# A two-layer graph network on one core: 391 edge tiles in place of 392, and gathers spread differently among the scatters

## The chip, the cores and the metric

The kernel runs on one core of a Trainium2 chip. The metric is the device time of one execution in microseconds. The kernel before has a median of 2975.88 us over three runs (2974.57 to 2979.17).

## The reference

A graph with 100000 nodes of 64 features and 50000 edges, sorted by their target `dst`. Two layers, each with a residual and a layer norm:

```python
def _L0_gnn_ref(features, src, dst, edge_weight, W1, W2, b1, b2):
    messages = features[src] * edge_weight[:, None]
    aggregated = jax.ops.segment_sum(messages, dst, num_segments=N_NODES)
    act = lambda x: jax.nn.leaky_relu(x, negative_slope=LEAKY_ALPHA)
    out = act(features * aggregated @ W1 + b1) + act(aggregated @ W2 + b2)
    sq = jnp.sum(out * out, axis=1, keepdims=True)
    return out * jax.lax.rsqrt(jnp.maximum(sq, L2_EPS))

def _L1_gnn_ref(x, edges, edge_weights, ...):
    node_indices, neighbour_indices = (edges[0], edges[1])
    messages = _ffn(x[neighbour_indices], W1p, b1p, W2p, b2p) * edge_weights[:, None]
    agg = jax.ops.segment_sum(messages, node_indices, num_segments=num_nodes)
    out = _ffn(jnp.concatenate([x, agg], axis=1), W1u, b1u, W2u, b2u)
    sq = jnp.sum(out * out, axis=-1, keepdims=True)
    return out * jax.lax.rsqrt(jnp.maximum(sq, EPS_L2))

edge_index = jnp.stack([src, dst])
x = _layernorm(x + _L0_gnn_ref(x, src, dst, ...), axis=-1)
x = _layernorm(x + _L1_gnn_ref(x, edge_index, edge_weight, ...), axis=-1)
```

The first layer gathers by `src` and adds by `dst`; the second gathers by `dst` and adds by `src`.

## The kernel before

**Tiles and windows.** A tile is 128 edges, one a partition. Four tiles (WT) are a window. 50000 edges fill 390 tiles (EC) and 80 edges of one more, so 391 tiles hold edges; the kernel rounds up to 98 windows (NWIN), 392 tiles. Windows are counted from 0 to 97 here, tiles from 0 to 391. The padding edges of the last tile carry weight 0 and are scattered to rows outside the result. Node rows are worked in chunks of 1024 (CR), also 98 (NCH).

**Three stages**, each a block with a barrier at its end. `first_edges` makes the edge sums of the first layer. `second_edges` computes the first layer's node rows, 8 groups of a chunk and the 4 gathered tiles of a window together, and from the latter the messages and edge sums of the second layer. `last_rows` computes the second layer's node rows.

**First edge stage.** POOL sends one indirect DMA for each tile (`gather`, line 243), which fetches 128 rows of x into the big tile `xg`. DVE builds matrices `weigh` that join edges of a window with the same target (`equal_rows`, lines 368 and 374), PE applies them (`join`, line 300), ACT evicts the sums into a ring of three buffers `ms` (`take`, line 323), and POOL adds them to the table in HBM with one accumulating indirect DMA for each tile (`scatter`, line 256). Scatter k waits for take k and for the landing of scatter k-1 (all four DMAs); take k waits for the landing of scatter k-3. Before its loop, POOL sends EARLY = 112 gathers and waits until SP's DMAs have cleared the table (`zeroed3`). Then it runs through the windows: scatter k, and then the gathers from upto(k) to upto(k+1):

```python
def upto(k):
    return min(EARLY + (TILES - EARLY) * k // (NWIN - 4), TILES)
```

PE's join k waits for the gathers of its window, which are counted in pairs of windows after the first 28 (`arrival`).

**Second edge stage.** POOL sends the gathers of 8 windows (LEAD), then for each k scatter k (line 546) and the four gathers of window k+8 (line 532), as long as there are any. A gather fills a slot of the ring `box` (6 slots, SB), and the first of a window waits until the slot's former rows are added. The other engines work in rounds; in round t:

```python
for t in range(ROUNDS):
    of(t, 2, sum_outputs)
    ...
    of(t, 2, sum_centred)
    of(t, 0, multiply)
```

is DVE's list, where `of(t, lag, what)` does window t-lag. `multiply` (line 731) is the first step on a window: it waits for the window's gathers and for SP's load of the chunk. PE turns and multiplies it one round later, and the window's take (line 691) comes five rounds after. So take k and multiply k+4 are near each other in time, and take k needs multiply k+3. Here too take k waits for the landing of scatter k-3, and scatter k for take k and for the landing of scatter k-1.

Of the kernel before, what the change touches and what calls it, by code (L numbers as in the profile page):

```python
# [39 lines left out]
def gnn_kernel(nc, x, src, dst, edge_weight, w1a, w2a, b1a, b2a, w1p, b1p, w2p, b2p, w1u, b1u, w2u, b2u, out):  # L40
# [6 lines left out]
    assert EC < TILES  # L47
# [5 lines left out]
    EARLY = 28 * WT  # L53
# [29 lines left out]
    with ctx:  # L83
# [42 lines left out]
        def first_edges():  # L126
            c = ExitStack()
            with c:
# [30 lines left out]
                def arrival(k):  # L159

                    if k < COARSE:
                        return k // 4, 16 * WT * 4
                    pair = (k - COARSE) // 2
                    of = min(2, NWIN - COARSE - 2 * pair)
                    return COARSE // 4 + pair % RING, 16 * WT * (2 * (pair // RING) + of)
# [22 lines left out]
                with nc.Block(no_gpsimd_drain=True) as block:  # L188
# [52 lines left out]
                    def _(pool):  # L241
# [35 lines left out]
                        pool.wait_ge(scattered, 16 * TILES)  # L277
# [67 lines left out]
                    def _(dve):  # L345
# [96 lines left out]
        def second_edges():  # L442
            c = ExitStack()
            with c:
# [48 lines left out]
                with nc.Block(no_gpsimd_drain=True) as block:  # L493
# [31 lines left out]
                    def _(pool):  # L525
                        def gather(i, h):

                            if h == 0:
                                wait(pool, added, i - SB + 1)
                            for b in range(JOIN * h, JOIN * (h + 1)):  # L530
                                at = i * WT + b
                                pool.indirect_dma_start(out=box[i % SB][:, b, :, :].rearrange("p a f -> p (a f)"), out_offset=None,  # L532
                                                        in_=table_rows[:, :],
                                                        in_offset=bass.IndirectOffsetOnAxis(ap=node[1][:, at:at + 1], axis=0),
                                                        ).then_inc(gathered[i % SB], 16)

                        def scatter(k, h):
# [6 lines left out]
                            for b in range(JOIN * h, JOIN * (h + 1)):  # L544
                                at = k * WT + b
                                pool.indirect_dma_start(out=state[:, :], out_offset=bass.IndirectOffsetOnAxis(ap=sidx[1][:, at:at + 1], axis=0),  # L546
# [3 lines left out]
                        for i in range(LEAD):  # L550
                            for h in range(HALVES):
                                gather(i, h)
                        for k in range(NWIN):
                            for h in range(HALVES):
                                scatter(k, h)
                                if k + LEAD < NWIN:
                                    gather(k + LEAD, h)
                        for h in range(HALVES):
                            pool.wait_ge(scattered[h], 16 * JOIN * NWIN)
# [156 lines left out]
                    def _(dve):  # L716
# [326 lines left out]
```

## Time and profile before

| What | Value |
|---|---|
| Median of three runs | 2975.88 us |
| The profiled execution | 2982.28 us |
| its span in the profile | 2980.5 us |
| First edge stage | 0 to 1270 us |
| Second edge stage | 1273 to 2578 us |
| Last stage | 2580 to 2980 us |
| POOL, DVE, PE busy | 2361.0, 2211.5, 2150.9 us |

Times in the timeline are microseconds from the start of the span: the first number of a row is the start, the second the duration, and in brackets stands the idle time just before with what ended it. "issue" is a pause that nothing in the profile explains. POOL's duration of an indirect DMA is the making of its descriptors, not its landing; the landing shows in whoever waits for it. In the groups by line, a row gives busy time and mean nanoseconds of one, then the idle time before. In the windows, a row gives each engine's busy time and instructions in a stretch, the granted TensorE clock as a share of 2.4 GHz, and the DMA engines' share.

### The profile page before, as it was taken

The numbers are of one execution on the slowest core, as the hardware profiler recorded it, in microseconds if no ns is written. First come the engines' busy times: TensorE is split into PE (matmuls) and PEld (weight loads), VectorE is DVE, ScalarE is ACT, GpSimd is POOL, SyncE is SP. The second block draws the span as 40 slices with busy tenths as digits, with TensorE's granted clock in tenths as the row PEclk, the third lists the DMA queues.
The fourth block names the chain that finished last, engine by engine and source line by source line (L and its number), as shares of the span: only waits on it lengthen the run. The fifth ranks groups of instructions, "written<-read, shape, count | busy, mean of one in ns | idle before, by whom it ended". The sixth has DMA issues, their size and how long they took to land. (4 is left out here: it accounts for less than half of the span.)

```text
span 2980.5 us, 39234 instructions
## 1 busy us (share of the span) xinstructions
PE 2150.9 (72%) x11956; PEld 1675.4 (56%) x11956; DVE 2211.5 (74%) x5627; ACT 1070.7 (36%) x1964; POOL 2361.0 (79%) x1774
## 2 busy tenths in 40 slices
PE   4036555555555554269999999989999998599997
PEld 3035555555554544247777666666666666366664
DVE  5079888888888886457778777777777777188888
ACT  0000000000000000035555455545555554288887
POOL 7777888888888888758888888888888887488888
PEclk8555555555555555579999999999999999699998
DMA  9998888888888767467787777777777776356664
GB/s 228 206 204 187 180 173 177 175 183 177 176 180 170 158 141 151 83 175 179 186 187 184 169 166 176 180 176 159 178 178 169 170 175 123 79 196 207 206 209 156
DMA packets 1036087, 516.48 MB, mean 173 GB/s; under 512 B 540544, under 2 KB 998336, under 8 KB 1035880
## 3 DMA queue, kind: packets, MB, share of 16 engines
q1 hardware_dynamic: 764616, 372.57, 47.6%
q0 software_dynamic: 144256, 77.17, 19.2%
q10 hardware_dynamic: 127008, 64.23, 7.6%
q8 instruction: 99, 1.62, 0.2%
q14 instruction: 108, 0.88, 0.1%
HBM read 269.97 MB, written 243.84 MB: 172 GB/s over the span
## 5 line engine op out<-in xcount | busy, mean ns | idle before, releaser
L300 PE MATMUL sums<-xg,weigh 128*128 128x64 f32 x1960 | 437.7, 420 | 514.8 <-ACT ms L323 358.7
L546 POOL DMA_INDIRECT state<-ms,sidx x392 | 630.8, 1609 | 145.2 <-issue 116.9
L256 POOL DMA_INDIRECT table<-ms,sidx x392 | 622.2, 1587 | 142.2 <-issue 115.5
L300 PEld LDWEIGHTS sums<-xg,weigh 128*128 128x128 f32 x1960 | 423.2, 329 | 548.6 <-issue 471.5
L368 DVE TENSOR_SCALAR weigh<-rowp,key,ew 128x128 f32<-128x128 f32 (+3 forms) x784 | 423.9, 602 | 167.9 <-PE rowp L288 160.7
L532 POOL DMA_INDIRECT box<-table,node_dst x392 | 401.9, 1025 | 130.0 <-issue 107.6
L243 POOL DMA_INDIRECT xg<-in_x,node_src x392 | 382.8, 976 | 120.8 <-issue 104.9
L323 ACT ACTIVATE ms<-sums 128x256 f32<-128x256 f32 x98 | 37.6, 384 | 1144.4 <-DMA table<-ms,sidx 1076.1
L374 DVE SCALAR_TENSOR_TENSOR seen<-rowp,key,earlier 128x128 f32<-128x128 f32 (+3 forms) x784 | 383.1, 544 | 0.0
L579 PE MATMUL z_p<-turned_s,wz 128*128 128x512 f32 x588 | 331.7, 647 | 24.9 <-ACT turned_s L652 20.8
L589 PE MATMUL o_p<-cenz,leaky 128*128 128x65 f32 x2352 | 285.1, 278 | 27.6 <-DVE leaky L737 27.2
L589 PEld LDWEIGHTS o_p<-cenz,leaky 128*128 128x128 f32 x2352 | 272.9, 193 | 48.3 <-DVE leaky L737 48.2
L288 PE MATMUL rowp<-ident,key 128*128 128x128 f32 x784 | 186.4, 418 | 129.2 <-DVE seen L374 122.0
L625 PEld LDWEIGHTS ffo<-g,weigh_in 128*128 128x128 f32 x1960 | 238.3, 195 | 48.0 <-issue 47.3
L658 ACT ACTIVATE leaky<-z_p,bz 128x512 f32<-128x512 f32 x294 | 202.0, 687 | 129.6 <-PE z_p L579 119.3
L288 PEld LDWEIGHTS rowp<-ident,key 128*128 128x128 f32 x784 | 166.8, 241 | 129.9 <-DVE seen L374 122.8
L625 PE MATMUL ffo<-g,weigh_in 128*128 128x64 f32 x1960 | 234.4, 276 | 1.6 <-issue 1.6
L737 DVE SCALAR_TENSOR_TENSOR leaky<-z_p,bz,leaky 128x512 f32<-128x512 f32 x294 | 217.9, 741 | 21.6 <-ACT leaky L658 21.3
L570 PEld LDWEIGHTS turned_p<-ident,box 128*128 128x128 f32 x1176 | 154.6, 155 | 131.5 <-issue 80.3
L870 POOL TENSOR_TENSOR inv<-ssq,mhalf 128x8 f32<-128x8 f32 x98 | 161.0, 1642 | 74.4 <-DVE ssq L975 74.4
L570 PE MATMUL turned_p<-ident,box 128*128 128x128 f32 x1176 | 180.9, 296 | 48.0 <-DVE box L731 48.0
L742 DVE TENSOR_REDUCE v<-sq_y 128x12 f32<-128x768 f32 x98 | 93.4, 953 | 157.5 <-ACT sq_y L669 157.5
(94 smaller groups left out, 3549.6 us busy)
## 6 DMA issues: line engine op xcount, KB each, us to landing
box<-table SPq DMA_DIRECT2D x97, 768.0 KB, 5.3
joins<-weigh ACTq DMA_DIRECT2D x98, 640.0 KB, 3.8
weigh_in<-joins SPq DMA_DIRECT2D x98, 640.0 KB
table<-rows SPq DMA_DIRECT2D x97, 512.0 KB, 5.4
pair<-state SPq DMA_DIRECT2D x97, 512.0 KB, 3.8
xin<-in_x SPq DMA_DIRECT2D x97, 256.0 KB, 6.1
state<-y SPq DMA_DIRECT2D x97, 256.0 KB, 7.7
out<-y SPq DMA_DIRECT2D x97, 256.0 KB, 2.2
```

What stands on the lines that cost most here:

```text
L243: pool.indirect_dma_start(out=xg[:, i, :], out_offset=None, in_=x[:, :], in_offset=bass.IndirectOffsetOnAxis(ap=node[0][:, i:i + 1], axis= ...
L256: pool.indirect_dma_start(out=table[:, :], out_offset=bass.IndirectOffsetOnAxis(ap=sidx[0][:, i:i + 1], axis=0), in_=ms[k % MR][:, b, :], ...
L288: last = pe.transpose(rowp[n][k % 2][:, b * P:(b + 1) * P], key[n][:, i:i + 1].to_broadcast([P, P]), ident[:, :])
L300: last = pe.matmul(sums[k % 2][:, a * D:(a + 1) * D], block_of(0, k, b)[:, a * P:(a + 1) * P], xg[:, k * WT + b, :], start=b == a, stop=b ...
L368: last = dve.tensor_scalar(block_of(n, k, b), rowp[n][k % 2][:, (b + 1 - m) * P:(b + 1) * P], key[n][:, i:i + 1], ew[:, i:i + 1], ALU.is_e ...
L374: last = dve.scalar_tensor_tensor(out=seen[b][:, 0:m * P], in0=rowp[n][k % 2][:, (b + 1 - m) * P:(b + 1) * P], scalar=key[n][:, i:i + 1], ...
L532: pool.indirect_dma_start(out=box[i % SB][:, b, :, :].rearrange("p a f -> p (a f)"), out_offset=None, in_=table_rows[:, :], in_offset=bass ...
L546: pool.indirect_dma_start(out=state[:, :], out_offset=bass.IndirectOffsetOnAxis(ap=sidx[1][:, at:at + 1], axis=0), in_=ms[k % SM][:, b, :] ...
L570: last = pe.transpose(turned_p[n % 2][:, g * P:(g + 1) * P], box[i % SB][:, 4 * q + g, 0:2, :].rearrange("p a f -> p (a f)"), ident[:, :])
L579: pe.matmul(z_p[n % 2][:, :], wz[:, :], turned_s[q][:, :], start=True, stop=True).then_inc(z_up, 1)
L589: last = pe.matmul(o_p[:, b, g * M8:(g + 1) * M8], leaky[i % 2][r // 4][:, r % 4 * P:(r % 4 + 1) * P], cenz[:, :], start=True, stop=True)
L625: last = pe.matmul(ffo[:, (WT + a) * D:(WT + a + 1) * D], weigh[i % SW][:, at * P:(at + 1) * P], g2[i % 2][:, b * D:(b + 1) * D], start=b ...
```

## The change

The last tile, which holds no edges, is neither gathered nor scattered in either stage (`FILLED` = 391, `MISSING` = 1). The semaphore counts that wait for it are lowered. Its place in `xg` is set to zero by one DVE memset at the start of the kernel. EARLY goes from 112 to 120. In the first stage `upto` divides by NWIN - 3 in place of NWIN - 4, and in the second stage, which sent all four gathers of window k+8 after scatter k, a like `upto` spreads the remaining 359 gathers over 92 windows in place of 90.

```diff
+    FILLED = EC + (ER > 0)
+    MISSING = TILES - FILLED
...
-    EARLY = 28 * WT
+    EARLY = 30 * WT
...
-                            return min(EARLY + (TILES - EARLY) * k // (NWIN - 4), TILES)
+                            return min(EARLY + (TILES - EARLY) * k // (NWIN - 3), FILLED)
...
-                            for b in range(WT):
-                                i = k * WT + b
+                            for i in range(k * WT, min((k + 1) * WT, FILLED)):
+                                b = i % WT
...
+                        if MISSING:
+                            dve.memset(xg[:, FILLED:TILES, :], 0.0)
...
-                        def gather(i, h):
-
-                            if h == 0:
+                        def gather(at):
+
+                            i, b = divmod(at, WT)
+                            if b == 0:
                                 wait(pool, added, i - SB + 1)
...
+                        def upto(k):
+                            return min(LEAD * WT + (FILLED - LEAD * WT) * k // (NWIN - 6), FILLED)
...
                         for k in range(NWIN):
                             for h in range(HALVES):
                                 scatter(k, h)
-                                if k + LEAD < NWIN:
-                                    gather(k + LEAD, h)
+                            for at in range(upto(k), upto(k + 1)):
+                                gather(at)
...
-                            dve.wait_ge(gathered[s], 16 * WT * (i // SB + 1))
+                            dve.wait_ge(gathered[s], 16 * (WT * (i // SB + 1) - (MISSING if i == NWIN - 1 else 0)))
```

The end of POOL's list in the first stage, from scatter 93 on, before. A row is a run of equal instructions; xg is filled by gathers, table by scatters:

```order
199 L256 DMA table<-ms_0,sidx 300640x64 x4
200 L243 DMA xg<-in_x,node_src 128x64 x3
201 L256 DMA table<-ms_1,sidx 300640x64 x4
202 L256 DMA table<-ms_2,sidx 300640x64 x4
203 L256 DMA table<-ms_0,sidx 300640x64 x4
204 L256 DMA table<-ms_1,sidx 300640x64 x4
```

The same place now:

```order
199 L259 DMA table<-ms_0,sidx 300640x64 x4
200 L246 DMA xg<-in_x,node_src 128x64 x3
201 L259 DMA table<-ms_1,sidx 300640x64 x4
202 L246 DMA xg<-in_x,node_src 128x64 x2
203 L259 DMA table<-ms_2,sidx 300640x64 x4
204 L259 DMA table<-ms_0,sidx 300640x64 x4
205 L259 DMA table<-ms_1,sidx 300640x64 x3
```

Two gathers stand after scatter 94, where none stood; scatters 95, 96 and 97 end the list, and the last has three DMAs. In the loop 14 windows are followed by two gathers (0, 7, 14, 21, 29, 36, 43, 51, 58, 65, 73, 80, 87, 94), where two were (0 and 47); the others by three.

The end of POOL's list in the second stage, from scatter 88 on, before; box is filled by gathers, state by scatters:

```order
384 L546 DMA state<-ms_1,sidx 200640x64 x4
385 L532 DMA box<-table,node_dst 128x192 x4
386 L546 DMA state<-ms_2,sidx 200640x64 x4
387 L532 DMA box<-table,node_dst 128x192 x4
388 L546 DMA state<-ms_0,sidx 200640x64 x4
389 L546 DMA state<-ms_1,sidx 200640x64 x4
390 L546 DMA state<-ms_2,sidx 200640x64 x4
391 L546 DMA state<-ms_0,sidx 200640x64 x4
392 L546 DMA state<-ms_1,sidx 200640x64 x4
393 L546 DMA state<-ms_2,sidx 200640x64 x4
394 L546 DMA state<-ms_0,sidx 200640x64 x4
395 L546 DMA state<-ms_1,sidx 200640x64 x4
```

And now, from scatter 89 on:

```order
387 L555 DMA state<-ms_2,sidx 200640x64 x4
388 L536 DMA box<-table,node_dst 128x192 x4
389 L555 DMA state<-ms_0,sidx 200640x64 x4
390 L536 DMA box<-table,node_dst 128x192 x4
391 L555 DMA state<-ms_1,sidx 200640x64 x4
392 L536 DMA box<-table,node_dst 128x192 x4
393 L555 DMA state<-ms_2,sidx 200640x64 x4
394 L555 DMA state<-ms_0,sidx 200640x64 x4
395 L555 DMA state<-ms_1,sidx 200640x64 x4
396 L555 DMA state<-ms_2,sidx 200640x64 x4
397 L555 DMA state<-ms_0,sidx 200640x64 x4
398 L555 DMA state<-ms_1,sidx 200640x64 x3
```

The last gathers stand after scatter 91 in place of 89. To fill those two places, windows 0, 10, 20, 30, 40, 51, 61, 71 and 81 are followed by three gathers, so that each gather stands 1 (after window 0) to 9 tiles (after window 81) later in the list than before.

## Rows read from the trace of the kernel before

**Rows 1.** The page, busy time of each engine.

```profile
PE 2150.9 (72%) x11956; PEld 1675.4 (56%) x11956; DVE 2211.5 (74%) x5627; ACT 1070.7 (36%) x1964; POOL 2361.0 (79%) x1774
```

**Rows 2.** Windows: busy time in two stretches of the second edge stage.

```profile
1400.00:1600.00 200.00, 189.54 (x1209) 144.06 (x1209) 159.61 (x361) 109.53 (x200) 161.42 (x124) 1.00 0.79 183
...
2545.00:2555.00 10.00, 8.44 (x30) 6.27 (x29) 0.00 (x0) 1.63 (x4) 6.80 (x5) 0.50 0.28 16
```

**Rows 3.** Groups by line: POOL's gathers and scatters of both stages.

```profile
L546 POOL DMA_INDIRECT state<-ms,sidx x392 | 630.8, 1609 | 145.2 <-issue 116.9 <-DMA state<-ms,sidx 15.2 <-ACT ms L691 13.1
L256 POOL DMA_INDIRECT table<-ms,sidx x392 | 622.2, 1587 | 142.2 <-issue 115.5 <-DMA table<-ms,sidx 9.7 <-ACT ms L323 8.8
L532 POOL DMA_INDIRECT box<-table,node_dst x392 | 401.9, 1025 | 130.0 <-issue 107.6 <-DMA state<-ms,sidx 11.3 <-DVE y L780 8.5
L243 POOL DMA_INDIRECT xg<-in_x,node_src x392 | 382.8, 976 | 120.8 <-issue 104.9 <-DMA table<-ms,sidx 14.3 <-DMA node_src<-in_src 1.6
```

**Rows 4.** Timeline of POOL: the last early gather and the first scatter.

```profile
143.39 0.95 POOL L243 DMA_INDIRECT xg<-in_x,node_src  x1 [0.31 <-issue]
152.56 1.64 POOL L256 DMA_INDIRECT table<-ms,sidx  x1 [8.23 <-DMA table<-zeros]
```

**Rows 5.** Timeline of POOL around window 47, and ACT's take of window 50.

```profile
702.98 1.55 POOL L256 DMA_INDIRECT table<-ms,sidx  x1 [0.30 <-issue]
...
706.16 0.98 POOL L243 DMA_INDIRECT xg<-in_x,node_src  x1 [0.30 <-issue]
708.29 1.62 POOL L256 DMA_INDIRECT table<-ms,sidx  x1 [1.14 <-ACT ms L323]
...
707.57 0.38 ACT L323 ACTIVATE ms<-sums 128x256 f32<-128x256 f32 x1 [11.75 <-DMA table<-ms,sidx]
```

**Rows 6.** Timelines: last scatter of window 68, and ACT's take of window 71.

```profile
942.35 1.55 POOL L256 DMA_INDIRECT table<-ms,sidx  x1 [0.30 <-issue]
...
946.81 0.39 ACT L323 ACTIVATE ms<-sums 128x256 f32<-128x256 f32 x1 [11.63 <-DMA table<-ms,sidx]
```

**Rows 7.** Timelines: last gather, PE's join of window 96, first bare gap.

```profile
1233.45 0.95 POOL L243 DMA_INDIRECT xg<-in_x,node_src  x1 [0.30 <-issue]
...
1240.39 1.55 POOL L256 DMA_INDIRECT table<-ms,sidx  x1 [0.30 <-issue]
1244.26 1.55 POOL L256 DMA_INDIRECT table<-ms,sidx  x1 [2.32 <-DMA table<-ms,sidx]
...
1236.99 4.50 PE L300 MATMUL sums<-xg,weigh 128*128 128x64 f32 x20 [16.54 <-issue]
```

**Rows 8.** Timelines of POOL and DVE: a scatter and a multiply that meet.

```profile
1710.86 2.30 POOL L546 DMA_INDIRECT state<-ms,sidx  x1 [0.30 <-issue]
...
1710.71 0.95 DVE L731 TENSOR_TENSOR box<-box 128x768 f32<-128x768 f32 x1
```

**Rows 9.** Timeline of POOL: last gather of window 93, scatters 91, 92, 97 begin.

```profile
2449.75 1.32 POOL L532 DMA_INDIRECT box<-table,node_dst  x1 [0.30 <-issue]
...
2513.81 1.55 POOL L546 DMA_INDIRECT state<-ms,sidx  x1 [3.37 <-ACT ms L691]
...
2523.59 1.55 POOL L546 DMA_INDIRECT state<-ms,sidx  x1 [2.30 <-DMA state<-ms,sidx]
...
2571.15 1.55 POOL L546 DMA_INDIRECT state<-ms,sidx  x1 [2.40 <-DMA state<-ms,sidx]
```

**Rows 10.** Timelines: DVE's multiplies of windows 93 and 97, takes 90, 91, 97.

```profile
2465.72 0.95 DVE L731 TENSOR_TENSOR box<-box 128x768 f32<-128x768 f32 x1
...
2515.18 0.95 DVE L731 TENSOR_TENSOR box<-box 128x768 f32<-128x768 f32 x1
...
2476.30 0.38 ACT L691 ACTIVATE ms<-ffo 128x256 f32<-128x256 f32 x1 [1.49 <-PE ffo L625]
...
2487.70 0.38 ACT L691 ACTIVATE ms<-ffo 128x256 f32<-128x256 f32 x1 [1.49 <-PE ffo L625]
...
2555.09 0.38 ACT L691 ACTIVATE ms<-ffo 128x256 f32<-128x256 f32 x1 [4.64 <-DMA state<-ms,sidx]
```

More of the change, by code:

```diff
@@ L46, in gnn_kernel @@
     TILES = NWIN * WT
-    assert EC < TILES
+    FILLED = EC + (ER > 0)
+    MISSING = TILES - FILLED
+    assert EC < TILES and MISSING < WT
     NCH = -(-N // CR)
@@ L164, in arrival @@
                     of = min(2, NWIN - COARSE - 2 * pair)
-                    return COARSE // 4 + pair % RING, 16 * WT * (2 * (pair // RING) + of)
+                    missing = MISSING if COARSE + 2 * pair + of == NWIN else 0
+                    return COARSE // 4 + pair % RING, 16 * (WT * (2 * (pair // RING) + of) - missing)
                 gathered = [sem(f"gathered0_{q}") for q in range(COARSE // 4 + RING)]
@@ L276, in _ @@
                                 gather(i)
-                        pool.wait_ge(scattered, 16 * TILES)
+                        pool.wait_ge(scattered, 16 * FILLED)
                     @block.tensor
@@ L525, in _ @@
                     def _(pool):
-                        def gather(i, h):
-                            if h == 0:
+                        def gather(at):
+                            i, b = divmod(at, WT)
+                            if b == 0:
                                 wait(pool, added, i - SB + 1)
[L530 to L535, printed above, removed]
+                            pool.indirect_dma_start(out=box[i % SB][:, b, :, :].rearrange("p a f -> p (a f)"), out_offset=None,
+                                                    in_=table_rows[:, :],
+                                                    in_offset=bass.IndirectOffsetOnAxis(ap=node[1][:, at:at + 1], axis=0),
+                                                    ).then_inc(gathered[i % SB], 16)
+                        def upto(k):
+                            return min(LEAD * WT + (FILLED - LEAD * WT) * k // (NWIN - 6), FILLED)
                         def scatter(k, h):
@@ L545, in scatter @@
                                 at = k * WT + b
+                                if at >= FILLED:
+                                    break
                                 pool.indirect_dma_start(out=state[:, :], out_offset=bass.IndirectOffsetOnAxis(ap=sidx[1][:, at:at + 1], axis=0),
@@ L548, in scatter @@
                                                         ).then_inc(scattered[h], 16)
-                        for i in range(LEAD):
-                            for h in range(HALVES):
-                                gather(i, h)
+                        for at in range(LEAD * WT):
+                            gather(at)
                         for k in range(NWIN):
@@ L555, in _ @@
                                 scatter(k, h)
-                                if k + LEAD < NWIN:
-                                    gather(k + LEAD, h)
+                            for at in range(upto(k), upto(k + 1)):
+                                gather(at)
                         for h in range(HALVES):
-                            pool.wait_ge(scattered[h], 16 * JOIN * NWIN)
+                            pool.wait_ge(scattered[h], 16 * (JOIN * NWIN - (MISSING if h == HALVES - 1 else 0)))
                     @block.tensor
```

## The prediction

> **What bounds the kernel now.** I read the busy line of the page first: POOL 79% of the span, ahead of DVE and PE [rows 1]. That average hides stages with different limits, so I went on to the groups of POOL's instructions [rows 3], and then to POOL's timeline. In both edge stages its instructions follow one another with 0.30 us between them. In [rows 3] the idle time is nearly all "issue", the fixed pause. The other engines wait: in the first edge stage ACT's take of window 50 stood waiting for a scatter to land [rows 5]. So both stages last as long as POOL's list of gathers and scatters, plus the places where it stops. In the second stage PE is close behind, 189.5 of 200 us busy at the full clock, 2.4 GHz [rows 2].
>
> Prices on POOL, duration plus pause: a scatter 1.59+0.30 = 1.9 us, a gather in the loop 0.98 to 1.03+0.30 = 1.3 us [rows 3], an early one 0.95+0.31 = 1.25 us [rows 4]. After a window's four scatters the next window must wait until they have landed. Where gathers stand between, they hide it. Where none do, the gap is 2.3 us instead of 0.3 [rows 7, 9].
>
> **First stage, the start.** POOL ends its early gathers at 144.33 and waits 8.23 us for the clearing of the table; scatter 0 starts at 152.56 [rows 4]. Eight more early gathers take 8 x 1.25 = 10.0 us: they fill the wait, and scatter 0 starts at 144.33+10.0+0.3 = 154.6, **+2.1 us**. Their 8 x 32 KB beside the clearing cannot make it later than that by much. The new DVE memset of 128x64 values is small and off POOL's path: nothing.
>
> **First stage, the loop.** 280 gathers become 271: 9 x 1.27 = **-11.4 us**. One scatter goes: **-1.9 us**. Before, the gaps ahead of scatters 95, 96 and 97 are bare; now only those ahead of 96 and 97: **-2.0 us**. Against this, windows followed by two gathers in place of three rise from 2 to 14. Two gathers leave a gap of 2.9 us, three 4.2. Is 2.9 enough? After window 47 (two gathers) scatter 48 started 3.76 us after the last scatter's end, since the landing took 3.04 us [rows 5]. I compared each take with the end of the scatter that it waited for: in windows 11, 14, ... to 68, twenty in all, the landing took 2.7 to 3.2 us (47 and 68 are in [rows 5, 6]), in the other forty about 1.7. Of the 14 windows, 14, 29 and 65 fall on slow places: 3 x 0.84 = **+2.5 us**. If none were slow it is 0, if all were 11.8. I take 2.5, as the pattern repeats strictly in this run. Sum of the stage: 2.1-11.4-1.9-2.0+2.5 = **-10.7 us**.
>
> Is the later last gather on the path? Before, it ends at 1234.40 and PE's join starts at 1236.99, 2.6 us on [rows 7]. Now the last gather stands second after scatter 94, so it lands 5.2 us after that scatter's end; join (4.5 us) and take (0.4 us) are done at 10.1. Scatter 96 can start only at 2.9+7.2+2.3 = 12.4. It stays hidden, by 2.3 us.
>
> **Second stage, POOL's own list.** One gather and one scatter fewer: -1.3-1.9. Bare gaps fall from seven to five: 2 x 2.0 = -4.0 (the first of them was 3.37 us long [rows 9], which I take for noise). Together **-7.2 us**.
>
> **Second stage, what the spreading costs.** Nine windows are now followed by three gathers instead of four, so the gathers fall behind the scatters: 1 tile late after window 0, up to 9 tiles late in windows 82 to 92. Who waits for them? DVE's multiply. Before, the last gather of window 93 ended at 2451.07 [rows 9] and its multiply ran at 2465.72 [rows 10]: 14.6 us, less a landing of some 2.6 us, so 12 us to spare. The last tile of a window, four tiles late, comes 4x1.3+4x1.9 = 12.7 us later, nine tiles late 12 scatters and 9 gathers = 34 us. So from about window 31 on DVE, and behind it PE and ACT, will wait for gathers. POOL itself feels it only when the take comes after the scatter wants it. Before, take 91 ended at 2488.08 and scatter 91 started at 2513.81 [rows 9, 10]: 25.7 us ahead. Slipping by 34-12 = 22 us leaves about 4 us. That hides it through window 93.
>
> Not at the very end. Count from the end of scatter 91. The last gather of window 96 ends at +1.3 and lands at +3.9; multiply 96; multiply 97 one round of 11.4 us later (the takes at 2476.30 and 2487.70 [rows 10]), at +15.3. From multiply 97 to the end of take 97 went 2515.18 to 2555.47 = 40.3 us [rows 10]: take 97 is done at +55.6. POOL wants scatter 97 at 5.4+7.2+2.3+4x9.5 = +52.9 (9.5 is the step of the bare windows [rows 9]). It waits **+3 us** in all, between 0 (a landing of 1.7 us and shorter last rounds) and 7 (a landing near 6 us).
>
> **What hits POOL from DVE.** Scatter 1710.86 took 2.30 us instead of 1.6: DVE's multiply had started at 1710.71 and ran 0.95 us [rows 8]. A POOL instruction that starts inside a multiply is held until it ends. Undisturbed, the four gathers of a window average 0.975 and the scatters 1.58, so [rows 3] holds (1.025-0.975)x392 + (1.609-1.58)x392 = 31 us of it. In the new kernel the multiply starts when a gather lands, so it has another phase to POOL. At random, 8 starts in 12.7 us meet a multiply with chance 0.6 and lose 0.48 us on average: 0.285 x 98 = 28 us, **-3 us**. The bounds are far apart: none hit, -31; three of four window positions hit nearly in full (0.7 us each) over 75 windows, +26. I take the random value, since the last gather's place in its window moves through all four.
>
> The Trainium skill (SBUF — State Buffer, section Who interferes with whom) says that a DVE instruction with two SBUF inputs contends with GpSimd's reads, but infers that it does not stall descriptor generation. The held scatter above speaks for the first and against the inference; by the inference this term would be zero and the time 2961.
>
> **Sum.** -10.7-7.2+3-3 = -17.9 us. The profiled execution (span 2980.5, time 2982.28) would become 2964.4. It lies 6.4 us above the median of the runs, 2975.88; that gives **2958 us**. The third stage gains and loses nothing.
>
> **Rivals.** (1) *Gathers do not gate the rounds*, since landing is faster or rounds have more slack. Then the tail wait and the new phase fall away: -10.7-7.2 = -17.9, again 2958; it cannot be told apart by time, but by DVE's waits. (2) *The first stage returns nothing beyond its tile*: landings there are slow behind every second gather (up to +9.3), and the backlog after the start, where gaps of 6 us stand, eats 3 more: about 2970. The strict 1.7/3.0 pattern speaks against it. (3) *The late gathers reach POOL*. If multiply to take needs 4 us more than the 9 of now, because PE falls to 1.2 GHz as it did at the end (clock 0.50 [rows 2]), POOL pays 4 us in each 18 us of its last 110 before the bare windows, and 10 more in the tail: 6x4+10 = 34, which gives 2992, and 2975 at half of it. PE's steady load speaks against. (4) *Slower: multiplies lock onto POOL's starts.* Every multiply follows a landing at a fixed delay; were that delay 1.4 to 1.6 us, the next gather or scatter starts just inside it in three positions of four. +26 in place of -3: 2987. It decides from a held time of 0.5 us per window up; at 0.316 now, that takes a delay that never varies, and landings vary from 1.6 to 3. (5) *Multiplies miss POOL*: a held time near 0.05: 2938.
>
> **How the numbers follow.** Forecast with rival 1: 0.70. (2) 0.08. (3) 0.06, a third of it slower. (4) 0.06, half of it slower. (5) 0.10. The range of 8 in 10 goes from 2940 to 2972: low by half of (5), high by (2). 0.2% is 6 us, about what can be told from no change. Faster than 2970: forecast, (5) and half of (2), 0.84; within 6 us: the other half of (2), two thirds of (3), half of (4), 0.11; slower 0.05.
>
> **What would show it.** Right: scatter 0 near 154.6 with 0.30 ahead of it; two bare gaps and then the end of the first stage 10 to 11 us earlier; two-gather windows with 2.9 us gaps, three or four of them 3.8; in the second stage DVE waiting for box gathers from about window 31, POOL waiting for takes only in the last four windows, 3 us; POOL's gathers and scatters there at means near 1.02 and 1.61. Wrong: POOL idle for ACT's take before window 93, scatter means above 1.65, or a first stage that ends less than 7 us earlier.

## The result and the profile after

| | before | after |
|---|---|---|
| Median of seven runs each | 2977.62 us (2973.13 to 2979.47) | 2964.23 us (2961.78 to 2967.57) |
| Ratio, 95% interval | | 0.9958 (0.9948 to 0.9967) |
| Profiled execution, its span | 2982.28, 2980.5 us | 2967.57, 2965.8 us |
| Scatter 0 starts | 152.56 | 154.18 |
| Last scatter of the first stage ends | 1270.32 | 1262.31 |
| Second stage, first gather to end of last scatter | 1305.29 us | 1298.96 us |

The kernel is 13.4 us (0.4%) faster by the medians; 17.9 were forecast. The two spans differ by 14.7: 8.0 from the first edge stage, 6.3 from the second, and 0.3 from the last stage and the seams.

POOL's groups of the changed kernel, which answer to [rows 3] (busy us, mean ns, then the idle time before them):

```profile
L555 POOL DMA_INDIRECT state<-ms,sidx x391 | 635.1, 1624 | 148.6 <-issue 116.5 <-ACT ms L699 29.0 <-DMA state<-ms,sidx 3.2
L259 POOL DMA_INDIRECT table<-ms,sidx x391 | 622.3, 1592 | 136.4 <-issue 114.6 <-ACT ms L326 16.8 <-DMA table<-ms,sidx 4.7
L536 POOL DMA_INDIRECT box<-table,node_dst x391 | 388.2, 993 | 129.7 <-issue 107.3 <-DVE y L788 10.0 <-DMA state<-ms,sidx 9.8
L246 POOL DMA_INDIRECT xg<-in_x,node_src x391 | 380.7, 974 | 120.5 <-issue 105.8 <-DMA table<-ms,sidx 13.1 <-DMA node_src<-in_src 1.7
```

See first what changed most: the second stage's gathers fell from a mean of 1025 to 993 ns, its scatters rose from 1609 to 1624, and the scatters' idle time moved from "DMA state" (landings, the bare gaps) to "ACT ms" (takes), 13.1 to 29.0 us.

The start, POOL's timeline, answers to [rows 4]:

```profile
152.93 0.95 POOL L246 DMA_INDIRECT xg<-in_x,node_src  x1 [0.30 <-issue]
154.18 1.64 POOL L259 DMA_INDIRECT table<-ms,sidx  x1 [0.30 <-issue]
```

The 8.23 us of waiting are gone, filled with early gathers, as forecast (154.6).

The end of the first stage, POOL's timeline, answers to [rows 7]. The last gather now stands behind scatter 94, with three windows of scatters after it and two bare gaps:

```profile
1236.69 0.98 POOL L246 DMA_INDIRECT xg<-in_x,node_src  x1 [0.30 <-issue]
...
1247.60 1.55 POOL L259 DMA_INDIRECT table<-ms,sidx  x1 [2.38 <-DMA table<-ms,sidx]
...
1257.04 1.55 POOL L259 DMA_INDIRECT table<-ms,sidx  x1 [2.32 <-DMA table<-ms,sidx]
```

In the second stage, DVE's waits and the first of those that the late gathers cause, at window 33:

```profile
DVE box L739 <- DMA box<-table,node_dst: 89.7, 21, 24.8
...
1676.49 0.96 DVE L739 TENSOR_TENSOR box<-box 128x768 f32<-128x768 f32 x1 [2.81 <-DMA box<-table,node_dst]
```

Before, the multiply waited once, at the stage's start, for 35.4 us. Now it waits 21 times.

The tail of the second stage, POOL's timeline, answers to [rows 9], with ACT's takes of windows 92 and 97 and DVE's last multiply behind it ([rows 10]):

```profile
2488.10 0.95 POOL L536 DMA_INDIRECT box<-table,node_dst  x1 [0.30 <-issue]
2489.35 0.95 POOL L536 DMA_INDIRECT box<-table,node_dst  x1 [0.30 <-issue]
...
2502.00 0.95 POOL L536 DMA_INDIRECT box<-table,node_dst  x1 [0.30 <-issue]
2503.26 1.62 POOL L555 DMA_INDIRECT state<-ms,sidx  x1 [0.30 <-issue]
...
2514.11 1.55 POOL L555 DMA_INDIRECT state<-ms,sidx  x1 [3.63 <-ACT ms L699]
2515.97 1.88 POOL L555 DMA_INDIRECT state<-ms,sidx  x1 [0.30 <-issue]
...
2526.33 1.55 POOL L555 DMA_INDIRECT state<-ms,sidx  x1 [4.77 <-ACT ms L699]
...
2537.91 1.55 POOL L555 DMA_INDIRECT state<-ms,sidx  x1 [4.45 <-ACT ms L699]
...
2548.56 1.55 POOL L555 DMA_INDIRECT state<-ms,sidx  x1 [3.52 <-ACT ms L699]
...
2558.63 1.55 POOL L555 DMA_INDIRECT state<-ms,sidx  x1 [2.95 <-ACT ms L699]
...
2502.04 0.38 ACT L699 ACTIVATE ms<-ffo 128x256 f32<-128x256 f32 x1 [1.49 <-PE ffo L633]
...
2557.98 0.38 ACT L699 ACTIVATE ms<-ffo 128x256 f32<-128x256 f32 x1 [4.64 <-PE ffo L633]
...
2515.47 0.95 DVE L739 TENSOR_TENSOR box<-box 128x768 f32<-128x768 f32 x1
```

The take of window 92 is done 0.84 us before its scatter starts; the lead was 23.1 us before. All five scatters behind it wait for ACT's take, 19.3 us together where five bare gaps of 2.33 would be 11.65: POOL loses **7.7 us**. The scatter at 2515.97 started 0.50 us after the multiply and took 1.88 us in place of 1.55: it was held for the rest of the multiply, as the one of [rows 8] was.

### The profile page after: what moved, and what is told of

Its sections match the earlier page's. It is cut to its first block and busy times, and to the rows that moved or that the text cites. A ratio compares the mean times of both kernels' runs of the same rounds, so it can differ in the third digit from the quotient of the medians.

```text
span 2965.8 us, 39231 instructions
## 1 busy us (share of the span) xinstructions
PE 2141.6 (72%) x11956; PEld 1669.1 (56%) x11956; DVE 2216.3 (75%) x5628; ACT 1071.0 (36%) x1964; POOL 2349.5 (79%) x1770
## 3 DMA queue, kind: packets, MB, share of 16 engines
q8 instruction: 99, 1.62, 0.2%
## 5 line engine op out<-in xcount | busy, mean ns | idle before, releaser
L555 POOL DMA_INDIRECT state<-ms,sidx x391 | 635.1, 1624 | 148.6 <-issue 116.5
L259 POOL DMA_INDIRECT table<-ms,sidx x391 | 622.3, 1592 | 136.4 <-issue 114.6
L536 POOL DMA_INDIRECT box<-table,node_dst x391 | 388.2, 993 | 129.7 <-issue 107.3
L587 PE MATMUL z_p<-turned_s,wz 128*128 128x512 f32 x588 | 339.1, 661 | 27.9 <-ACT turned_s L660 20.9
L660 ACT ACTIVATE turned_s<-turned_p 128x512 f32<-128x512 f32 x294 | 174.8, 595 | 86.3 <-PE turned_p L578 78.8
```

The costliest lines, as they stand in the source:

```text
L587: pe.matmul(z_p[n % 2][:, :], wz[:, :], turned_s[q][:, :], start=True, stop=True).then_inc(z_up, 1)
```

## The experiments

Three chips took part, and they don't give the kernel before the same time: 2978.18 us on the first (median of 20 runs; the change's own comparison gave 2977.62, and its profiles are set beside those of this chip), 2994.4 on the second (35), 3005.74 on the third (35). Each ratio below is against the kernel before on the same chip. Stage lengths are those of the profiled executions. "Stage 1" is the end of its last scatter, "stage 2" runs from its first gather to the end of its last scatter.

### Which part gives what (first chip)

**The tile alone**: 391 tiles, with gathers where they were.

```diff
-    EARLY = 30 * WT
+    EARLY = 28 * WT
-    return min(EARLY + (TILES - EARLY) * k // (NWIN - 3), FILLED)
+    return min(EARLY + (TILES - EARLY) * k // (NWIN - 4), FILLED)
-    return min(LEAD * WT + (FILLED - LEAD * WT) * k // (NWIN - 6), FILLED)
+    return min((LEAD + k) * WT, FILLED)
```

> The kernel before with the 392nd tile left out alone: 112 early gathers, the old spreading in both stages. Theory (POOL's list sets both edge stages, each instruction at its own price): one gather 1.3 and one scatter 1.9 us fewer in each stage, 3.2 + 3.2 = -6.4 us in all; the first stage ends near 1267.1, the second lasts about 1302.1 (before: 1270.3 and 1305.3). Rival (the last window's tile is hidden in the barrier and the drain of the stage): under 2 us in all. The held time of POOL's second-stage instructions stays near 31 us.

**The first stage's part**: the third of these edits alone, on the changed kernel, so that the second stage is the one of before less its tile.

> The first stage as changed, the second with the old spreading and without the 392nd tile. Theory (the stages add up, each keeps its own gain): the first stage ends near 1262.3 as in the changed kernel, the second lasts 1302.1; together -8.0 - 3.2 = -11.2 us against before. Rival (the second stage's gain of 6.3 us comes from its new start or from the first stage, not from its spreading): second stage near 1299, -14.3 us in all. If the spreading is what moves the phase of the multiplies, gathers of the second stage stay at a mean of 1025 ns here, else they fall to 993.

**The second stage's part**: the first two edits alone.

> The second stage as changed, the first with the old spreading, 112 early gathers and without the 392nd tile. Theory: first stage ends near 1267.1 (-3.2), second lasts near 1299.0 (-6.3): -9.5 us in all; DVE waits for box gathers from about window 33, gathers average near 993 ns and scatters 1624. Rival (the held time follows an accident of the start): the means lie elsewhere and the second stage between 1290 and 1312.

| Kernel | Median us | Ratio (95%) | Stage 1 | Stage 2 | Box gather, state scatter, mean ns |
|---|---|---|---|---|---|
| tile alone | 2972.38 | 0.9984 (0.9975 to 0.9993) | 1265.98 | 1301.78 | 1015, 1616 |
| first stage's part | 2969.67 | 0.9977 (0.9967 to 0.9987) | 1260.77 | 1303.08 | 1023, 1617 |
| second stage's part | 2966.69 | 0.9966 (0.9954 to 0.9978) | 1264.81 | 1295.38 | 993, 1617 |

The tile by itself is 5.8 us by the medians (2 to 7 by the interval), with no gather moved: one gather and one scatter less in each stage are 2x(1.3+1.9) = 6.4. So nearly half of the change's 13.4 us has nothing to do with the spreading.

One execution can't be read to the microsecond. The second stage of the third kernel is the changed one, instruction for instruction, and took 1295.38 us where the change's own profile has 1298.96; its tail waits are 18.2 us in place of 19.3, and its scatters are held for less (1617 ns in place of 1624).

The first stage ended at 1265.98 and 1264.81 with the old order, and at 1262.31 and 1260.77 (1264.04 in a kernel below) with the new one: averages 1265.4 and 1262.4. Early gathers and spreading return **3 us** there, not the 7.5 that were forecast beyond the tile (-10.7 against -3.2).

In the second stage the gathers' mean tells the held time apart, on this chip. It is 1025, 1015 and 1023 ns where the gathers stand as before, 993 to 995 where they are spread:

```profile
L536 POOL DMA_INDIRECT box<-table,node_dst x391 | 400.1, 1023 | 129.7 <-issue 106.4 <-DMA state<-ms,sidx 11.9 <-DVE y L788 8.8
```

```profile
L536 POOL DMA_INDIRECT box<-table,node_dst x391 | 388.4, 993 | 129.7 <-issue 106.3 <-DMA state<-ms,sidx 10.4 <-DVE y L788 10.3
```

The upper row is of the kernel with the first stage's part, the lower of that with the second stage's: 11.7 us less on the same 391 gathers.

### Is the tail's wait made by the lateness of the last gather? (first chip)

**Spreading that ends one window earlier.** Rival: the tail waits since PE runs at half its clock there, whatever stands before.

```diff
-    return min(LEAD * WT + (FILLED - LEAD * WT) * k // (NWIN - 6), FILLED)
+    return min(LEAD * WT + (FILLED - LEAD * WT) * k // (NWIN - 7), FILLED)
```

> The changed kernel with the second stage's gathers spread over 91 windows in place of 92 (NWIN - 7): each tile at most 5 places late and the last gather behind scatter 90. Theory (the 7.7 us that POOL loses before scatters 93 to 97 come from the last gather's lateness: landing 4.7, a round, and 43 us to take 97): the last gather is earlier by one scatter group, 7.5 us, so these waits fall to 0 to 1 us, and one bare gap of 2.0 us comes back: second stage shorter by about 5 us, near 1294, if the held time stays; the held time may move by 6 either way. Rival (the waits come from PE's half clock in the last rounds whatever the gathers do): waits of 4 us and more remain, second stage near 1299 to 1301.

Measured: **2959.85 us**, ratio 0.9937 (0.9923 to 0.995), the fastest kernel of the study on this chip. Stage 2 took 1291.89 us. POOL's timeline at its end, ACT's take of window 92, and a window of the tail (busy time of PE, its weight loads, DVE, ACT, POOL, then PE's clock):

```profile
2505.70 1.55 POOL L555 DMA_INDIRECT state<-ms,sidx  x1 [2.57 <-DMA state<-ms,sidx]
...
2515.23 1.55 POOL L555 DMA_INDIRECT state<-ms,sidx  x1 [2.37 <-DMA state<-ms,sidx]
...
2553.31 1.55 POOL L555 DMA_INDIRECT state<-ms,sidx  x1 [2.27 <-DMA state<-ms,sidx]
...
2492.97 0.38 ACT L699 ACTIVATE ms<-ffo 128x256 f32<-128x256 f32 x1 [1.49 <-PE ffo L633]
...
2535.00:2545.00 10.00, 8.44 (x31) 6.40 (x31) 0.00 (x0) 1.62 (x4) 6.63 (x5) 0.50 0.24 13
```

There are six bare windows now, one more than in the change, but each costs the bare 2.27 to 2.57 us, and none waits for ACT: the take of window 92 stands 12.4 us ahead of its scatter (2505.70 less 0.38 less 2492.97), where it stood 0.84 ahead. PE's clock in the tail is 0.50 here too. The rival falls, the lateness stands. One more bare gap (+2) has bought off the 7.7 us. The stage is shorter by 7.1 us than in one execution of the change's stage and by 3.5 than in the other, the medians differ by 4.4 (2964.23 and 2959.85), and the two intervals touch.

### Do DVE's multiplies hold POOL? (second chip)

Both kernels are the kernel before with one more DVE instruction of the same size and length ahead of each multiply. One reads two operands in SBUF, the other one. Both write a tile that nobody reads, so they compute in addition to the reference, and the output stays.

```diff
+    dve.tensor_tensor(spare[:, :, :], box[s][:, :, 0, :], box[s][:, :, 2, :], ALU.mult)
     dve.tensor_tensor(box[s][:, :, 1, :], box[s][:, :, 1, :], box[s][:, :, 0, :], ALU.mult).then_inc(multiplied, 1)
```

> The kernel before with one more DVE instruction ahead of each multiply of the second stage: a tensor_tensor of the same size (128x768, 0.95 us) with both inputs in SBUF, its result unused. Theory (a POOL instruction that starts inside a DVE instruction with two SBUF inputs is held to its end): twice as long a time in which starts are held, so the held time doubles from 30 us: POOL's second-stage gathers and scatters together grow by 20 to 40 us, and the second stage, which is POOL-bound, from 1305 to 1325 to 1345. Rival (the long POOL instructions have another cause that only falls near the multiply): no growth beyond 3 us, since DVE has the time to spare.

```diff
+    dve.tensor_reduce(spare[:, :], box[s][:, :, 0, :], AX_X, ALU.add)
     dve.tensor_tensor(box[s][:, :, 1, :], box[s][:, :, 1, :], box[s][:, :, 0, :], ALU.mult).then_inc(multiplied, 1)
```

> The same with a tensor_reduce of the same size in the same place, which has one SBUF input, its result unused. Theory: nothing is held by it, the second stage stays within 5 us of 1305 and POOL's means near 1025 and 1609 ns (the multiply's own holding may shift by some us). Rival (any DVE instruction there, or the longer DVE round, costs the time): as long as with the two-input instruction.

Measured: two operands 2994.89 us, ratio 1.0 (0.9978 to 1.0021), stage 2 1308.71; one operand 2984.59, 0.9965 (0.9944 to 0.9986), stage 2 1303.53. POOL's groups, two operands first:

```profile
L547 POOL DMA_INDIRECT state<-ms,sidx x392 | 634.7, 1619 | 156.2 <-issue 106.0 <-ACT ms L692 50.2
...
L533 POOL DMA_INDIRECT box<-table,node_dst x392 | 383.0, 977 | 137.5 <-issue 109.1 <-DVE y L782 16.3 <-DMA state<-ms,sidx 9.4
```

```profile
L547 POOL DMA_INDIRECT state<-ms,sidx x392 | 621.2, 1585 | 163.4 <-issue 98.1 <-ACT ms L692 65.3
L533 POOL DMA_INDIRECT box<-table,node_dst x392 | 382.9, 977 | 138.8 <-issue 109.1 <-DVE y L782 17.4 <-DMA state<-ms,sidx 9.4
```

Undisturbed, 392 scatters of 1.58 us are 619. With one operand they are 621.2, with two 634.7: 13.5 us more. The starts say it directly: 91 scatters start inside the added two-operand instruction and take 1.75 us on average, 89 start inside the added one-operand instruction and take 1.58. One window of the two-operand kernel, POOL and then DVE:

```profile
2018.56 1.80 POOL L547 DMA_INDIRECT state<-ms,sidx  x1 [0.30 <-issue]
...
2017.96 0.95 DVE L732 TENSOR_TENSOR spare<-box 128x768 f32<-128x768 f32 x1
2018.83 0.95 DVE L733 TENSOR_TENSOR box<-box 128x768 f32<-128x768 f32 x1
```

The scatter starts 0.60 us into the first instruction and is held into its rest of 0.35 us, but not through the second: 1.80 in place of 1.58 us, where a hold to 2019.78 would make it 2.8. POOL gets in between the two. Not always: one scatter that starts in the last 0.03 us of the first instruction takes 2.35 us, which is a hold through the second.

The two added instructions differ in more than their inputs: the one writes 768 values a partition, the other 12. The kernel before settles which it is. Its sum `y<-o_p,box` is a `tensor_tensor` of the multiply's size and length that writes 768 values into SBUF, but one of its inputs, `o_p`, is in PSUM. A scatter that starts 0.11 us into it keeps its length (POOL, then DVE):

```profile
1743.66 1.55 POOL L546 DMA_INDIRECT state<-ms,sidx  x1 [0.31 <-issue]
...
1743.55 0.94 DVE L780 TENSOR_TENSOR y<-o_p,box 128x768 f32<-128x768 f32 x1
```

In that kernel 52 gathers and 16 scatters start inside this sum, at least 0.1 us before its end; the longest take 1.03 and 1.62 us. Inside the multiply start 36 gathers and 36 scatters, with means of 1.52 and 1.93 us. Every gather above 1.1 us and every scatter above 1.66 us is among these, and the others have means of 0.976 and 1.577.

So two things are shown: it is an instruction with both inputs in SBUF that holds POOL, and one hold costs no more than the rest of that one instruction. Two things missed: neither the held time nor the stage grew as the theory had it, since the second instruction holds nobody who is already held, and since on this chip POOL's list alone didn't set the stage (below). With one operand the multiply runs 0.95 us later in its round, and from 1500 us on not one of 344 scatters is longer than 1.65 us (of 344 in the two-operand kernel 69 are): at that phase it misses them, which is the likely source of its gain. The kernel before has no profile on this chip to show it.

The rule in the Trainium skill (SBUF — State Buffer, section Who interferes with whom) that a DVE instruction with two SBUF inputs contends with GpSimd's reads agrees with 634.7 against 621.2; the inference there that descriptor making is not stalled doesn't, for these DMAs. All of them take their row numbers from a tile in SBUF (`sidx`, `node_dst`), so it may be that read which is held; whether a DMA of POOL without such a tile is held, no run here tells.

**The same doubled instruction on the third chip**, beside another copy of the kernel before:

> The kernel before with a second two-input DVE instruction ahead of each multiply, once more, with before_again from the same chip to set against it. Theory: POOL's second-stage instructions are busy 10 to 40 us longer than in before_again if POOL's list sets that stage (chip like the first), and about 13 us longer than with the one-input instruction if the rounds do, as in the second comparison. Rival: busy sums equal within 3 us.

> The kernel before, unchanged, for its profile on the chip of this comparison. On the chip of the second comparison the same kernel took 2994 us, 16 more than on the chip of the first. If this chip is like the first: first stage to 1270, second 1305, DVE's multiplies unhindered and POOL's take waits at the end only. If it is like the second: scatter 1 or 2 is held up by 10 to 20 us, and in the second stage POOL waits a few tenths for the take of every other window, because a round takes 12.8 us there where POOL needs 12.7.

| Third chip | Median us | Ratio (95%) | Stage 2 | Box gathers + state scatters, busy us |
|---|---|---|---|---|
| before, once more | 3003.46 | 1.0 (0.9987 to 1.0014) | 1317.96 | 382.1 + 641.9 |
| doubled, two operands | 3003.17 | 0.9988 (0.9975 to 1.0001) | 1318.20 | 383.4 + 637.7 |

The doubling did nothing, against what was expected: 1021.1 us busy with it, 1024.0 without. In the kernel before the scatters already have a mean of 1637 ns there: the phase of multiplies to POOL's starts is fixed on that chip, and one scatter in nearly every window is held (from 1500 to 2500 us 76 of 309 are longer than 1.65 us, 18 or more in each 250 us). So the held time can't be had by counting instructions; it is a matter of phase.

### What makes every third landing slow? (second chip)

SP issues two kinds of DMA that could stand beside a slow landing: the 1 MB clears of `state`, one in three steps, and the loads of a ring. The kernel with the clears one step earlier, on the changed kernel:

```diff
-    if c0 % 3 == 2 and c0 // 3 < len(later):
+    if c0 % 3 == 1 and c0 // 3 < len(later):
-    for piece in later[(NCH - 3) // 3 + 1:]:
+    for piece in later[(NCH - 2) // 3 + 1:]:
```

> The changed kernel with SP's 1 MB clears of state, one behind every third chunk, moved from chunks 2, 5, 8 to 1, 4, 7. In both kernels the scatters of windows 11, 14, ... 68 land in 2.7 to 3.2 us in place of 1.7. Theory (a clear is in flight beside them): the slow windows move to those with remainder 1, so the two-gather windows 43 and 58 get gaps near 3.7 and 14, 29, 65 fall to 2.9; the stage's end moves by under 1.5 us. Rival (the ring of three ms buffers, or what it implies): the slow windows stay at remainder 2.

Measured: 2992.07 us, ratio 0.9983 (0.9962 to 1.0005). POOL's timeline of the changed kernel behind window 14, and then of this one behind windows 14 and 43; two gathers stand in each of the three places:

```profile
331.21 0.98 POOL L246 DMA_INDIRECT xg<-in_x,node_src  x1 [0.30 <-issue]
333.14 1.62 POOL L259 DMA_INDIRECT table<-ms,sidx  x1 [0.95 <-ACT ms L326]
```

```profile
348.37 0.98 POOL L246 DMA_INDIRECT xg<-in_x,node_src  x1 [0.31 <-issue]
349.65 1.63 POOL L259 DMA_INDIRECT table<-ms,sidx  x1 [0.30 <-issue]
...
675.92 0.98 POOL L246 DMA_INDIRECT xg<-in_x,node_src  x1 [0.30 <-issue]
677.73 1.62 POOL L259 DMA_INDIRECT table<-ms,sidx  x1 [0.83 <-ACT ms L326]
```

The wait is gone from window 14 (also from 29 and 65) and stands at 43 and 58: from windows with remainder 2 by three to those with remainder 1. The slow landings (16: 3.69 us, 19: 2.87, 22: 3.86) move with it. This is not the chip: on this one the one-operand kernel, whose clears are not moved, has its slow landings at 17 (3.14 us) and 20 (3.07), remainder 2. The clears are the cause; the ring of loads and the ring of three `ms` buffers, which stayed where they were, are not.

### Would more gathers at the start pay? (second and third chip)

Five gathers behind windows 1 to 6 in place of three, two behind every third window from 24 on, with the second stage of the fastest kernel (and a ring of 14 semaphores for the arrivals in place of 12). The theory: gaps of 4 to 7 us stand there anyway, since takes are late, so gathers in them cost nothing.

```diff
-    return min(EARLY + (TILES - EARLY) * k // (NWIN - 3), FILLED)
+    return min(EARLY + sum(2 if j == 0 or j == 94 or (j >= 24 and j % 3 == 0) else 5 if j <= 6 else 3 for j in range(k)), FILLED)
```

> The kernel with the second stage over 91 windows, and in the first stage five gathers behind each of windows 1 to 6, where the landings take 5 to 6 us and POOL waits; in return two behind every third window from 24 on (remainder 0, away from the slow landings). Theory: the gaps behind windows 1 to 6 (33 us with three gathers) become 6.7 each, 40 us, twelve later gathers of 1.27 go: -15.2+6.9 = -8.3, and the three slow two-gather gaps go, -2.2: the first stage ends near 1254 instead of 1264, the whole near 2950. Rival (the backlog grows with the gathers, so the landings move out behind them): gaps of 9 us and more there, end near 1262.

Measured on the second chip: 2989.9 us, ratio 0.9974 (0.9953 to 0.9995), stage 1 1277.39. The comparison it needs was then made on the third chip:

> The front-loaded version once more, beside the one it starts from (second_91_again). Theory: five gathers behind windows 1 to 6 hide in landings of 5 to 6 us; on a chip like the first the first stage ends 8 to 10 us earlier than that of second_91_again. On a chip like the second, where POOL stood 10 and 18 us behind windows 1 and 2 for ACT's takes, the gathers there are free too, and the gain is again 6 to 10 us. Rival (more gathers make the backlog longer): gain under 3 us.

> The changed kernel with the second stage over 91 windows, once more, as the base of front_again. On a chip like the first: 16 to 19 us faster than before (ratio 0.9937 there), waits before the bare scatters at 2.3 to 2.6. On a chip like the second: less, since the rounds and not POOL's list set the second stage: 5 to 10 us.

| Third chip | Median us | Ratio (95%) | Stage 1 | Stage 2 |
|---|---|---|---|---|
| five gathers at the start | 2999.4 | 0.9981 (0.9966 to 0.9996) | 1277.64 | 1315.50 |
| three gathers (fastest of the first chip) | 3002.05 | 0.9988 (0.9977 to 0.9999) | 1279.85 | 1313.05 |

The first stage ends 2.2 us earlier, less than was expected. On this chip one gap is long, behind window 1 (17.22 us of waiting for ACT's take with three gathers, 18.14 with five); the gaps behind windows 2 to 6 are 4.2 to 4.9 us with three gathers, and 6.7 to 7.2 with five, so there the added gathers were paid for in full. The intervals of the two kernels overlap: no difference is shown.

### Why two of the chips gain less

On the second and third chip the rounds of PE, ACT and DVE are longer. Here is the stretch of [rows 2], first row, for the kernel before on the third chip: PE is busy for 174 of 200 us where it was 189.5, at the same clock.

```profile
1400.00:1600.00 200.00, 174.35 (x1103) 131.57 (x1102) 145.42 (x332) 97.80 (x181) 162.30 (x123) 1.00 0.76 174
```

and ACT's takes in it, of windows 43 to 46:

```profile
1904.64 0.38 ACT L691 ACTIVATE ms<-ffo 128x256 f32<-128x256 f32 x1 [1.49 <-PE ffo L625]
1917.41 0.38 ACT L691 ACTIVATE ms<-ffo 128x256 f32<-128x256 f32 x1 [1.49 <-PE ffo L625]
1930.37 0.38 ACT L691 ACTIVATE ms<-ffo 128x256 f32<-128x256 f32 x1 [1.49 <-PE ffo L625]
1943.23 0.38 ACT L691 ACTIVATE ms<-ffo 128x256 f32<-128x256 f32 x1 [1.49 <-PE ffo L625]
```

A round takes 12.7 to 13.1 us there, and in nearly every window the take is done only 0.28 to 0.46 us before its scatter starts. On the first chip rounds of 11.9 to 12.3 us at the start of the stage, shorter than POOL's own 12.8, carry the takes ahead of POOL, by nearly 30 us at window 27; from there the takes wait for POOL's scatters to land. The 189.5 of [rows 2] is of that first part and not of the whole stage: in the four stretches of 200 us behind it PE is busy for 181 to 185.

Does the round bind there? From the start of scatter 30 to that of scatter 85, all four kernels profiled on the third chip take 708.9 to 709.5 us, also the two with three gathers fewer in between. So a gather less on POOL is worth little in the loop, and this is why the fastest kernel returns 3.7 us on the third chip (3005.74 to 3002.05) and 18.3 on the first (2978.18 to 2959.85). Nor are the tail's waits gone there with the last gathers a window earlier: scatters 93 to 97 wait 19.4 us for their takes, since no lead has been built up. The longer stage of the kernel before (1317.96 against 1305.29) doesn't come from the loop either: scatters 30 to 85 take 709.1 us on the third chip and 713.5 on the first. It comes from the stretch before scatter 0 (+8.0) and from the one behind the start of scatter 85 (+12.3), where POOL could go faster and the takes don't let it; the loop gives 7.7 back. The instructions last as long there as elsewhere (a leaky 0.74 us on all three); the rounds are longer by waits among PE, ACT and DVE. What makes them is open; no run here tells it.

## Why the prediction was right, and where its steps missed

The direction and the range held, and most of the mechanism: POOL's list as the bound, the hidden last gather, the gated rounds, a wait at the end. The size was 4.5 us off by the medians (17.9 forecast, 13.4 measured), and 3.2 by the profiled executions (14.7). Several terms missed by more than that sum shows, and some of their misses cancel.

**The start** (+2.1): +1.6, right. **The last gather hidden**: right; scatter 96 waited for the landing (2.38 us) and no more. **Bare gaps of the first stage**: two, as forecast.

**Two-gather windows** (+2.5): windows 14, 29 and 65 had gaps of 3.56, 3.62 and 3.71 us, the others 2.9. But window 47 of the kernel before was such a slow window too (3.76, [rows 5]) and is none now, so the count should have been 2 x 0.84 = 1.7, and these windows gave 2.2-0.9 = +1.3. The rest is another thing: two landings of 3.75 and 4.26 us behind windows 44 and 59 made gaps of 4.47 and 4.98 where three gathers give 4.2 (so in all three kernels with the new order; why is open). Gaps that exceed the covered values in windows 12 to 69 sum to 3.3 us, against 0.8 to 1.0 in the kernels with the old order: +2.4, right in size by luck.

**The backlog after the start**: the step that failed in the first stage. It was put at nothing in the sum and stood, at 3 us, only in rival 2. POOL's idle time beyond its pauses of 0.30 us, from scatter 0 to scatter 12, sums to 7.6, 7.2 and 5.9 us in the three kernels with the old first stage and to 9.5, 8.4 and 9.6 in the three with the new. Three rows of POOL's timeline behind window 1 of the changed kernel show where:

```profile
173.62 0.98 POOL L246 DMA_INDIRECT xg<-in_x,node_src  x1 [0.30 <-issue]
174.90 0.94 POOL L246 DMA_INDIRECT xg<-in_x,node_src  x1 [0.30 <-issue]
178.79 1.62 POOL L259 DMA_INDIRECT table<-ms,sidx  x1 [2.94 <-ACT ms L326]
```

The gap behind window 1 grew from 4.17 to 6.80 us. Early gathers were moved ahead of scatter 0, into a wait; but what followed was a wait too, for takes, and taking fewer gathers behind windows there doesn't shorten it. That is +2.3 us by these averages, +1.8 between the two profiled executions, of the 2.7 by which this stage missed.

**The scatters' own length in the first stage**: one scatter fewer was to be -1.9 us, and the scatters' busy time stayed the same (622.2 us for 392, 622.3 for 391; 619.7 and 620.4 for the 391 of the two kernels with the old order). That is some +2 us which the sum lacks. What lengthens them was not looked into.

**POOL's list in the second stage** (-7.2): right; five bare windows in place of seven.

**Gathers gate the rounds**: right, from window 33 on (31 forecast), and rival 1 falls with it. POOL didn't wait for a take before window 93.

**The tail** (+3, bounds 0 to 7): **+7.7**, just outside. Take 97 was done at +60.5 us from the end of scatter 91, in place of +55.6, by two misses of like size. The landing of a box gather was taken as 2.6 us, as long as a join of the first stage stood behind its last gather ([rows 7]), and that gather's rows are a third as long (64 values in place of 192). From the end of a window's last gather to its multiply went 3.1 to 5.8 us in the 19 windows from 33 on whose multiply waited over 0.3 us for it, 4.90 in window 95, the last of them. With that, multiply 97 ran 17.6 us after the end of scatter 91 (15.3 forecast). And from multiply 97 to the end of take 97 went 42.9 us where 40.3 were carried over from the kernel before. The bound of a landing near 6 us named the first, and nothing named the second.

**Held time** (-3, bounds -31 and +26): by the groups, 31 us became (0.993-0.975)x391 + (1.624-1.58)x391 = 24.2, or **-6.8**. The gathers lost 12.6 of their 19.6 us, and the scatters gained 5.8. The number of hits was near the random one (0.6 x 98 = 59 forecast, 61 counted), but the phase isn't random: 13 gathers and 48 scatters start inside a multiply, of 391 each. That the sum came out near the value at random is in part luck. (The upper bound doesn't come out of its own terms either: 75 x 0.7 - 31 is +21.5.)

In sum, first stage -10.7 forecast and -8.0 measured, second -7.2+3-3 = -7.2 forecast and -7.2+7.7-6.8 = -6.3 measured. Rival 2 was half true (most of its 3 us of backlog, not its slow landings everywhere); rival 3 shows as a tail of 7.7 us in place of 10 and nothing before it; rivals 4 and 5 have no trace in the scatters' mean of 1624 ns, nor in the gathers' 993.

## What to carry to other kernels

When work is spread over a list that bounds a kernel, find the place where its lateness leaves the cover: here the last four tiles were needed one window earlier than the even spread gave them, and ending it one window earlier made the stage 3.5 to 7.1 us shorter. Work moved ahead into a wait at the start is only a gain as far as no other wait stands right behind it: of 10 us of gathers moved into an 8 us wait, the start itself took back 1.6, the waits for takes behind it 2.3 and the windows with fewer gathers 2.4. And a gain on one engine's list holds on a chip where that engine is the bound; the same kernel gave 18.3 us on one chip and 3.7 on another.

## What the runs showed of the hardware

- An indirect DMA's instruction on GpSimd that starts inside a DVE `tensor_tensor` with both inputs in SBUF is longer by about the rest of that instruction (1.88 us for 1.55 with 0.45 left, 1.80 for 1.58 with 0.35 left). Inside a `tensor_reduce` of the same length it isn't (89 scatters, 1.58 us on average), nor inside a `tensor_tensor` with one input in PSUM (52 gathers and 16 scatters, none above 1.03 and 1.62 us). Between two such DVE instructions in a row GpSimd mostly gets in.
- A landing beside a 1 MB clear takes 2.7 to 4.3 us in place of 1.7, and this follows the clear when that is moved by a step.
- The same kernel takes 2978, 2994 and 3006 us on three chips. On the first and the third, with PE at the same granted clock of 1.00 in the stretch compared (1400 to 1600 us), a round of the second stage takes 11.9 to 12.3 us on the one and 12.7 to 14.2 on the other. The durations of the instructions agree; the waits don't.
